# Routing the second feed-forward in segments of 20 and 12 token tiles

## Chip, cores and metric

One core of a Trainium2 chip. The metric is the device time of one execution in microseconds; the kernel before and the changed one run on the same chip, and the median of several runs counts.

## The reference

The input is 4096 tokens of 128 features. `x` goes through a macaron block:

```
x = x + 0.5 * ffn(layernorm(x))
x = x + attention(layernorm(x))
x = x + 0.5 * ffn(layernorm(x))
```

`ffn` is a mixture of 8 experts with top-2 gating:

```
weights = softmax(x @ gate_w.T + bias); top_w, top_i = top_k(weights, 2); top_w /= sum(top_w) + 1e-6
for e in range(8):
    h = gelu(x @ w_up[e].T)            # 128 -> 512
    out += sparse_w[..., e] * (h @ w_down[e].T)
out = layernorm(out) + x
```

`attention` is a causal linear attention (cosformer, 16 heads of 64, sequences of 1024 tokens) with ReLU features weighted by cos and sin of the position, a denominator, and an output projection.

## The kernel before

**Tiles.** 4096 tokens are 32 tiles of 128, or 8 blocks of 4 tiles. Tensors that the experts multiply are split into a high and a low f16 part.

**Segments.** Each feed-forward is routed in two segments of 16 tiles. Segments are numbered 0 and 1 (first feed-forward), 2 and 3 (second); even ones use `xs[0]`, `ys[0]` and half 0 of `slot_idx`, odd ones `xs[1]`, `ys[1]` and half 1. `gating` (L489) picks the two experts of each token in ten pieces (0 to 9) on VectorE, with an Exp on ScalarE after piece 0. `route_product` counts on TensorE, and `route` (L566), 20 operations on VectorE, computes where each (token, choice) goes, `slot_idx`, and which expert each tile of slots has, `tile_e`, packed three bits apiece into registers' words. `scatter` (L626) sends each tile's rows to DRAM `xs` in expert order, with two indirect DMAs a tile on GpSimd's queue. Each expert's rows are padded to 256, so a segment of 16 tiles (4096 rows) has 23 pairs of slot tiles, `NPAIR`.

**The pair loop.** For each pair, SP loads `xs` into one of three `xs_in` (L930), TensorE transposes it (L727), VectorE copies it (L824), TensorE multiplies (L742 to L744), ScalarE does gelu (L803) and the high part (L808), VectorE the low part (L828), TensorE the second product (L757 to L759), VectorE copies y into one of three `y_sb` (L835), SP stores it in `ys` (L936). SP's queue is in order: in iteration p it issues the load of pair p + 3 and then the store of pair p - 3. The loads of segment 1 or 3 start within the loop of the segment before, and the first of them waits for all scatters of its segment:

```
if p == 0:
    sp.wait_ge(scat[i % 2], 16 * 2 * HALF * (k + 1))
```

**After the pairs.** For each block q, GpSimd gathers each token's two rows from `ys` (`gather`, L665, eight indirect DMAs), VectorE combines and normalises (`combine`, L681 to L698), GpSimd takes the power (`finish_power`, L672), VectorE applies it and adds to x (`finish_apply`, L705, L710), SP stores the output. The blocks of segment 2 are done beside the pairs of segment 3 (combine in iterations 6, 10, 14, 18, apply in 9, 13, 17, 21); those of segment 3 after the last pair. `add_input` (L643) adds the normalised input to `x_tok` on GpSimd, one instruction per segment.

**Attention.** Blocks n = 0 to 7, each with 8 steps (hp = 0 to 7) of two heads. In each step GpSimd makes a low part of q (L1377, POOL), low parts of the state (L1380, L1381) and the products with cos and sin (L1359, two), VectorE multiplies scores by the decay (L1258), updates the state (L1271), makes the low part of the probabilities (L1275) and key features (L1233, `k_features`), and more. Other work is put into given steps by hand, in `beside` on VectorE and after the step on GpSimd:
- the layer norm before the second feed-forward of block n - 1 in steps 1 and 2 of block n, its transposes in 4 and its gate logits in 5;
- the gathers of the first feed-forward's last four blocks, one a step in blocks 0 to 3;
- the gating of segment 2 in block 5, its `route` in step 0 of block 6, its scatters from step 1 of block 6 to step 7 of block 7, one tile a step (two in the first).

The gating of segment 3 runs in iterations 4 to 8 of segment 2's pair loop, after block 7's layer norm, its `route` in iteration 10 and all its scatters behind that on GpSimd's queue.

## Time and profile before

| | |
|---|---|
| median of 3 runs | 1253.76 us (1251.31 to 1256.22) |
| profiled execution | 1257.42 us |
| its span, first to last instruction | 1255.5 us |
| busy: VectorE, TensorE, GpSimd, ScalarE | 1009.6, 928.8, 765.9, 707.3 us |
| mean granted clock of TensorE | 0.929 |
| attention, first L1377 to last | 288.5 to 993.8 us |
| second feed-forward, first low part to end | 1012.2 to 1255.5 us |

Times inside the execution are counted from the first instruction. The page calls the engines PE (TensorE), DVE (VectorE), ACT (ScalarE), POOL (GpSimd) and SP (SyncE). Share of busy time is a mean over stretches with different limits, so each stretch is read by itself. The row of a waiting instruction names, in brackets, how long its engine was idle and which instruction or DMA released it.

### The profile page before, as it was taken

The numbers are of one execution on the slowest core, as the hardware profiler recorded it, in microseconds if no ns is written. First come the engines' busy times: TensorE is split into PE (matmuls) and PEld (weight loads), VectorE is DVE, ScalarE is ACT, GpSimd is POOL, SyncE is SP. The second block draws the span as 40 slices with busy tenths as digits, with TensorE's granted clock in tenths as the row PEclk, the third lists the DMA queues.
The fourth block names the chain that finished last, engine by engine and source line by source line (L and its number), as shares of the span: only waits on it lengthen the run. The fifth ranks groups of instructions, "written<-read, shape, count | busy, mean of one in ns | idle before, by whom it ended". The sixth has DMA issues, their size and how long they took to land.

```text
span 1255.5 us, 32918 instructions
## 1 busy us (share of the span) xinstructions
PE 928.8 (74%) x12872; PEld 752.7 (60%) x12872; DVE 1009.6 (80%) x2109; ACT 707.3 (56%) x1014; POOL 765.9 (61%) x635
## 2 busy tenths in 40 slices
PE   3303988878988878878878988978979778859800
PEld 3302977766766656656656766756766667748700
DVE  7887786987889899899899898898888768538923
ACT  2112766657765755666765776746757646636600
POOL 2178736706867656757656565557987721767264
PEclk9999999989999998999999999988989989969955
DMA  9322424310000000000000000000000012234231
GB/s 336 128 109 73 141 79 111 103 47 6 8 9 8 8 6 8 8 7 8 8 6 2 2 2 2 2 2 19 14 14 13 21 53 72 95 97 122 77 93 50
DMA packets 69508, 61.77 MB, mean 49 GB/s; under 512 B 8304, under 2 KB 60016, under 8 KB 69104
## 3 DMA queue, kind: packets, MB, share of 16 engines
q1 hardware_dynamic: 60448, 42.64, 11.1%
q0 software_dynamic: 8192, 16.79, 4.3%
q8 instruction: 109, 1.79, 0.6%
q10 hardware_dynamic: 720, 0.23, 0.1%
q14 instruction: 39, 0.32, 0.1%
HBM read 30.80 MB, written 28.84 MB: 48 GB/s over the span
## 4 chain that ended last, share of the span: by engine, by line
DVE 30%; POOL 25%; PE 20%; issue 16%; ACT 6%; DMA 2%; DVEq 0%; POOLq 0%; SPq 0%
POOL xs L636 8%; POOL arena_a L1377 5%; DVE arena_b L1275 4%; POOL arena_a L1359 4%; DVE arena_a L1233 3%; PE bank L1043 3%; DVE arena_c L828 3%; ACT arena_c L1153 3%; POOL arena_b L665 2%; DVE arena_c L1271 2%; POOL arena_c L1381 2%; DVE xn_new L426 2%; DVE arena_b L1258 2%; PE bank L742 2%; DVE zt L705 2%
## 5 line engine op out<-in xcount | busy, mean ns | idle before, releaser
L636 POOL DMA_INDIRECT xs<-xhl,slot_idx x128 | 154.1, 1204 | 98.3 <-issue 57.2
L803 ACT ACTIVATE arena_c<-bank,s_pre 128x1024 f32<-128x1024 f32 x92 | 102.3, 1112 | 164.4 <-PE bank L744 158.9
L1377 POOL TENSOR_TENSOR arena_a<-arena_a 128x1024 f16<-128x1024 f32 x64 | 139.4, 2178 | 53.5 <-ACT arena_a L1153 52.9
L1359 POOL TENSOR_TENSOR arena_a<-arena_b,trig_rows 128x512 f32<-128x512 f32 x128 | 160.3, 1272 | 8.6 <-issue 8.6
L1153 ACT ACTIVATE arena_c<-arena_a 128x1024 f16<-128x1024 f32 x64 | 67.6, 1057 | 161.5 <-DVE arena_a L1233 161.5
L757 PE MATMUL bank<-wdn_hi,arena_c 128*128 x736 | 131.2, 222 | 31.8 <-DVE arena_c L828 31.8
L665 POOL DMA_INDIRECT arena_b<-ys,slot_idx x96 | 108.5, 1130 | 66.5 <-DMA ys<-arena_b 38.8
L828 DVE SCALAR_TENSOR_TENSOR arena_c<-arena_c,s_h 128x1024 f16<-128x1024 f32 x92 | 125.2, 1361 | 22.1 <-ACT arena_c L808 22.1
L758 PE MATMUL bank<-wdn_hi,arena_c 128*128 x736 | 131.2, 222 | 0.0
L759 PE MATMUL bank<-wdn_lo,arena_c 128*128 x736 | 131.0, 222 | 0.0
L1258 DVE TENSOR_TENSOR arena_b<-bank,decay 128x512 f32<-128x512 f32 x128 | 82.4, 686 | 41.0 <-PE bank L1043 40.4
L1153 ACT ACTIVATE arena_b<-arena_b 128x512 f16<-128x512 f32 x128 | 77.9, 630 | 63.9 <-DVE arena_b L1258 63.9
L808 ACT ACTIVATE arena_c<-arena_c,s_h 128x1024 f16<-128x1024 f32 x92 | 105.7, 1148 | 3.0
L742 PE MATMUL bank<-arena_b,wup_hi 128*128 128x256 f16 x368 | 103.9, 282 | 0.8
L743 PE MATMUL bank<-arena_b,wup_hi 128*128 128x256 f16 x368 | 103.8, 282 | 0.0
L744 PE MATMUL bank<-arena_b,wup_lo 128*128 128x256 f16 x368 | 103.7, 282 | 0.0
L1380 POOL TENSOR_TENSOR arena_c<-arena_c 128x130 f16<-128x130 f32 x64 | 35.6, 556 | 107.9 <-ACT arena_c L1203 107.6
L1275 DVE TENSOR_TENSOR arena_b<-arena_b 128x1024 f16<-128x1024 f32 x64 | 101.4, 1584 | 0.0
L1233 DVE SCALAR_TENSOR_TENSOR arena_a<-bank,trig_cols 128x512 f32<-128x512 f32 x128 | 82.3, 683 | 19.0 <-PE bank L969 18.0
L757 PEld LDWEIGHTS bank<-wdn_hi,arena_c 128*128 128x128 f16 x736 | 73.2, 99 | 35.2 <-issue 34.1
L967 PE MATMUL bank<-wo_hi,arena_c 128*128 128x128 f16 x256 | 49.4, 228 | 59.6 <-DVE arena_c L1242 59.5
L727 PE MATMUL bank<-ident_h,arena_b 128*128 128x128 f16 x368 | 37.5, 227 | 67.1 <-DMA arena_b<-xs 42.7
(227 smaller groups left out, 3762.8 us busy)
## 6 DMA issues: line engine op xcount, KB each, us to landing
arena_b<-xs SPq DMA_DIRECT2D x92, 128.0 KB
ys<-arena_b SPq DMA_DIRECT2D x92, 128.0 KB
xs<-arena_c SPq DMA_DIRECT2D x2, 3072.0 KB, 18.2
arena_a<-in_w_up SPq DMA_DIRECT2D x1, 2048.0 KB, 13.0
arena_b<-in_w_down SPq DMA_DIRECT2D x1, 2048.0 KB, 13.6
xs<-xhl,slot_idx POOLq DMA_INDIRECT x128, 2.3
out_x<-x_tok SPq DMA_DIRECT2D x8, 256.0 KB, 2.7
arena_b<-ys,slot_idx POOLq DMA_INDIRECT x96
```

Source lines behind the costliest of these rows:

```text
L636: nc.gpsimd.indirect_dma_start(d["xs"][half], bass.IndirectOffsetOnAxis(slot_idx[:, half, choice, t:t + 1], axis=0), xhl[:, half, t, :], N ...
L665: nc.gpsimd.indirect_dma_start(rows_of(q)[:, t, choice, :], None, d["ys"][half], bass.IndirectOffsetOnAxis(slot_idx[:, half, choice, at:at ...
L742: nc.tensor.matmul(dst, w_hi, x_hi, start=True, stop=False)
L757: nc.tensor.matmul(dst, hi, w_hi, start=(c + s == 0), stop=False, skip_group_check=True)
L758: nc.tensor.matmul(dst, lo, w_hi, start=False, stop=False, skip_group_check=True)
L759: i = nc.tensor.matmul(dst, hi, w_lo, start=False, stop=(c + s == CH), skip_group_check=True)
L828: nc.vector.scalar_tensor_tensor(h_lo[G % 4], h32[G % 2], s_h[:, 0:1], h_hi[G % 4], ALU.mult, ALU.subtract).then_inc(f["lo_done"], 1)
L1153: nc.scalar.activation(dst, src, ACT.Copy, scale=scale).then_inc(done, 1)
L1233: i = nc.vector.scalar_tensor_tensor(to[:, :, g, :], keys, 0.0, trig, ALU.max, ALU.mult)
L1275: nc.vector.tensor_tensor(probs_lo, probs, probs_hi, ALU.subtract).then_inc(a["probs_lo_done"], 1)
L1359: i = nc.gpsimd.tensor_tensor(q_trig[h], q_relu[h], trig_rows[:, bass.ds(u * BLK, BLK)], ALU.mult)
L1377: nc.gpsimd.tensor_tensor(q_lo, arena_a[:, 0:2 * BLK], q_hi, ALU.subtract).then_inc(a["q_lo_done"], 1)
```

## The change

The four segments get sizes of their own, in blocks 4, 4, 5, 3. The second feed-forward's segment 2 has 20 tiles and 27 pairs, segment 3 has 12 tiles and 19 pairs; the sum of pairs stays 46. Everything that was written with `HALF` or `NPAIR` uses `SEG_TILES`, `PAIRS` and `FIRST_PAIR`. The tables of `route` grow from 24 to 32 entries, and the zeroed scratch in DRAM from 24 to 28 pairs of tiles a half. The constants of routing stay in one SBUF tensor and aren't copied apart.

In attention, piece 0 of segment 2's gating moves from step 0 to step 6 of block 5 (block 4's gate logits must be in), the other pieces to steps 0 to 3 of block 6, `route` to step 4 of block 6, and the scatters to two tiles (four DMAs) a step from step 5 of block 6 to step 6 of block 7. In the pair loop, the fifth block of segment 2 is combined in iteration 22 of segment 3 and applied in iteration 25; three blocks are left for the end. TensorE waits for the last copy of y before it starts the attention.

```diff
-SLOTS, NPAIR, NTABLE = 24 * 2 * P, 23, 24
+SEG_BLOCKS = (4, 4, 5, 3)
+SEG_TILES = tuple(TPB * n for n in SEG_BLOCKS)
+SEG_START = (0, SEG_TILES[0], 0, SEG_TILES[2])
+SEG_END = (4, 8, 13, 16)
+PAIRS = tuple(n + E - 1 for n in SEG_TILES)
+FIRST_PAIR = (0, PAIRS[0], PAIRS[0] + PAIRS[1], sum(PAIRS[:3]), sum(PAIRS))
+SLOTS, NTABLE, WIDEST = 28 * 2 * P, 32, max(SEG_TILES)
...
             if j == 0:
-                v.wait_ge(gate_read, NBLK // 2 * (i + 1))
+                v.wait_ge(gate_read, SEG_END[i])
...
-        def spread(p, lag):
-            return p >= lag and (p - lag) % 4 == 0 and (p - lag) // 4 < NBLK // 2
+        def spread(p, lag, i):
+            return p >= lag and (p - lag) % 4 == 0 and (p - lag) // 4 < SEG_BLOCKS[i - 1]
...
             if k:
-                for q in range(NBLK + EARLY, 2 * NBLK):
+                for q in range(SEG_END[2], SEG_END[3]):
                     combine(v, q)
                     finish_apply(v, q)
...
                 ln_power(g, 1, NBLK - 1)
                 add_input(g, 2)
-                scatter(g, 3, range(0, HALF))
+                scatter(g, 3, range(0, SEG_TILES[3]))
                 add_input(g, 3)
+                for i in (2, 3):
+                    first = SEG_END[i] - SEG_BLOCKS[i]
+                    gather(g, first)
+                    for q in range(first + 1, SEG_END[i]):
+                        gather(g, q)
+                        finish_power(g, q - 1)
+                    finish_power(g, SEG_END[i] - 1)
...
                 if p == 0:
-                    sp.wait_ge(scat[i % 2], 16 * 2 * HALF * (k + 1))
+                    sp.wait_ge(scat[i % 2], 16 * 2 * (SEG_TILES[i] + (SEG_TILES[i - 2] if i > 1 else 0)))
...
             pe.wait_ge(w_att_ready, 1)
+            pe.wait_ge(f["y_used"], FIRST_PAIR[2])
...
-                if n == 5:
-                    for j in ((0,), (), (1, 2), (3, 4), (5, 6), (7,), (8,), (9,))[hp]:
+                if n == 5 and hp == 6:
+                    gating(v, 2, 0)
+                if n == 6 and hp < 4:
+                    for j in ((1, 2), (3, 4, 5), (6, 7), (8, 9))[hp]:
                         gating(v, 2, j)
-                if n == 6 and hp == 0:
+                if n == 6 and hp == 4:
                     route(v, 2)
...
-                        at = 8 * (n - 6) + hp - 1
-                        if at >= 0:
-                            scatter(g, 2, (at + 1,) if at else (0, 1))
+                        at = 2 * (NHP * (n - 6) + hp - 5)
+                        if 0 <= at < SEG_TILES[2]:
+                            scatter(g, 2, range(at, min(at + 2, SEG_TILES[2])))
...
-            nc.vector.tensor_copy(slot_tile[:], route_raw[:, 0:at])
-            nc.vector.tensor_copy(keep[:].rearrange("p e t -> p (e t)"), route_raw[:, at:at + E * NTILE // 2])
-            nc.vector.tensor_copy(below_b[:], route_raw[:, at + E * NTILE // 2:at + E * NTILE // 2 + P])
-            nc.vector.tensor_copy(digit[:], route_raw[:, at + E * NTILE // 2 + P:]).then_inc(const_ready, 1)
+            nc.vector.tensor_copy(below_b[:], below).then_inc(const_ready, 1)
```

## Rows read from the trace of the kernel before

**Rows 1.** Windows: stretch, length, busy us (instructions) by engine, clock, DMA.

```profile
288.50:363.40 74.90, 71.66 (x1126) 54.08 (x1123) 61.41 (x113) 57.34 (x96) 60.61 (x49) 1.00 0.03 8
...
734.20:820.70 86.50, 75.76 (x1142) 57.70 (x1142) 77.80 (x150) 60.48 (x104) 50.98 (x43) 0.98 0.01 2
820.70:917.30 96.60, 80.00 (x1172) 60.52 (x1169) 86.33 (x154) 59.93 (x102) 73.00 (x58) 0.93 0.03 12
917.30:993.80 76.50, 66.56 (x993) 50.80 (x991) 67.39 (x115) 51.62 (x88) 63.31 (x53) 0.96 0.04 14
...
1012.20:1090.20 78.00, 65.52 (x819) 59.32 (x817) 58.82 (x118) 51.52 (x48) 28.68 (x22) 0.93 0.25 75
```

**Rows 2.** Timeline of POOL, one step of block 6: start, us, engine, line.

```profile
877.02 2.15 POOL L1377 TENSOR_TENSOR arena_a<-arena_a 128x1024 f16<-128x1024 f32 x1
...
883.97 1.83 POOL L636 DMA_INDIRECT xs<-xhl,slot_idx  x1
886.11 0.96 POOL L636 DMA_INDIRECT xs<-xhl,slot_idx  x1 [0.30 <-issue]
887.09 2.13 POOL L1377 TENSOR_TENSOR arena_a<-arena_a 128x1024 f16<-128x1024 f32 x1
```

**Rows 3.** Waits of SP's queue: us in total, times, longest.

```profile
SPq L930 <- DMA xs<-xhl,slot_idx: 35.7, 2, 26.0
```

**Rows 4.** Timeline of VectorE from segment 2 to 3.

```profile
1087.28 1.28 DVE L828 SCALAR_TENSOR_TENSOR arena_c<-arena_c,s_h 128x1024 f16<-128x1024 f32 x1 [0.23 <-ACT arena_c L808]
...
1090.15 1.28 DVE L828 SCALAR_TENSOR_TENSOR arena_c<-arena_c,s_h 128x1024 f16<-128x1024 f32 x1 [0.56 <-ACT arena_c L808]
1109.95 0.42 DVE L835 COPY arena_b<-bank 128x256 f32<-128x256 f32 x1 [18.52 <-DMA ys<-arena_b]
...
1121.85 1.28 DVE L828 SCALAR_TENSOR_TENSOR arena_c<-arena_c,s_h 128x1024 f16<-128x1024 f32 x1 [1.68 <-ACT arena_c L808]
```

**Rows 5.** Timeline of VectorE from segment 0 to 1, same operations.

```profile
184.08 1.28 DVE L828 SCALAR_TENSOR_TENSOR arena_c<-arena_c,s_h 128x1024 f16<-128x1024 f32 x1 [0.57 <-ACT arena_c L808]
...
196.55 1.29 DVE L828 SCALAR_TENSOR_TENSOR arena_c<-arena_c,s_h 128x1024 f16<-128x1024 f32 x1 [1.68 <-ACT arena_c L808]
```

**Rows 6.** Timeline of VectorE near the end of segment 3.

```profile
1179.12 0.87 DVE L681 TENSOR_SCALAR zt<-arena_b,w 128x128 f32<-128x128 f32 x4
...
1182.52 0.17 DVE L698 TENSOR_SCALAR fvar<-fmv 128x4 f32<-128x4 f32 x1
...
1188.96 1.11 DVE L705 TENSOR_SCALAR zt<-zt,fmv,frstdh 128x128 f32<-128x128 f32 x4
...
1194.04 0.42 DVE L835 COPY arena_b<-bank 128x256 f32<-128x256 f32 x1 [1.38 <-PE bank L759]
```

**Rows 7.** Timeline of POOL: first gathers of the first and the last block.

```profile
1197.09 1.02 POOL L665 DMA_INDIRECT arena_b<-ys,slot_idx  x1 [13.32 <-DMA ys<-arena_b]
...
1229.42 1.01 POOL L665 DMA_INDIRECT arena_b<-ys,slot_idx  x1 [0.18 <-issue]
```

**Rows 8.** Timeline of VectorE in block 6: first and last of route, then L1275.

```profile
825.76 0.28 DVE L581 COPY rt_tot<-bank 128x128 f32<-128x128 f32 x1
...
833.71 0.17 DVE L605 CAST tile_e<-rt_pack 128x3 int32<-128x3 f32 x1
...
852.43 7.43 DVE L1275 TENSOR_TENSOR arena_b<-arena_b 128x1024 f16<-128x1024 f32 x1
```

**Rows 9.** Line L1275 over the whole span: duration ns min/median/max.

```profile
L1275 DVE TENSOR_TENSOR arena_b<-arena_b x64: 1212/1216/7435, 291.9 to 994.6; 128x1024 f16<-128x1024 f32 x64
```

**Rows 10.** Timeline of POOL: scatters 1, 24 and 32 of segment 3.

```profile
1061.53 1.99 POOL L636 DMA_INDIRECT xs<-xhl,slot_idx  x1 [40.80 <-DVE tile_e L605]
...
1095.10 0.96 POOL L636 DMA_INDIRECT xs<-xhl,slot_idx  x1 [0.30 <-issue]
...
1105.18 0.96 POOL L636 DMA_INDIRECT xs<-xhl,slot_idx  x1 [0.30 <-issue]
```

**Rows 11.** Timeline of VectorE at the start of the second feed-forward.

```profile
1016.30 5.29 DVE L426 TENSOR_SCALAR xn_new<-x_tok,mv,rstdh 128x128 f32<-128x128 f32 x4
```

More of the change, by code:

```diff
@@ L880, in ffn_pool @@
         def ffn_pool(g, k):
-            def finishing(q, power, norm):
-                gather(g, q)
-                if power is not None:
-                    finish_power(g, power)
-                if k == 0 and norm is not None:
-                    ln_power(g, 0, norm % 8)
             if k == 0:
@@ L891, in ffn_pool @@
                 reduce_largest(g, 2, 9, 2)
[L892 to L893 removed]
+                scatter(g, 0, range(10, SEG_TILES[0]))
+                scatter(g, 1, range(0, SEG_TILES[1]))
                 add_input(g, 0)
                 add_input(g, 1)
+                gather(g, 0)
+                for q in range(1, EARLY):
+                    gather(g, q)
+                    finish_power(g, q - 1)
+                    if q > 1:
+                        ln_power(g, 0, q - 2)
+                ln_power(g, 0, EARLY - 2)
+                finish_power(g, EARLY - 1)
+                ln_power(g, 0, EARLY - 1)
             else:
```

258 lines of the change are left out of this document (127 added, 131 removed).

## Prediction

> **What bounds the kernel now.** I read the table of windows first, then the chain of waits, then the timelines of GpSimd (POOL) and VectorE (DVE) around the places that the diff touches. Three stretches matter, and each has another limit.
>
> The attention runs 8 blocks of 8 steps. A block without gating, layer norm or scatters takes 74.9 us, so 9.4 us a step; block 5, which carries the gating of segment 2, takes 86.5, block 6, with its routing and 16 scatters, 96.6, and the first seven steps of block 7 take 76.5 [rows 1]. In the steps with two scatters the chain of waits stays on POOL without a gap: one step is 10.07 us from one subtraction L1377 to the next, and the scatters start 6.95 us into it [rows 2]. So POOL sets the pace there.
>
> The second feed-forward loses most at the change from segment 2 to 3. SP waited up to 26.0 us in one piece for scatters before it could issue a load [rows 3], and the stores queue behind that load. VectorE's low part of pair 21 starts at 1090.15, the first of segment 3 at 1121.85, with an 18.52 us wait for a store in between [rows 4]. The same passage in the first feed-forward, where the scatters were long done, takes 196.55 - 184.08 = 12.5 us [rows 5]. So 31.7 - 12.5 = 19.2 us are a stall.
>
> The last stretch is the gathers of four blocks on POOL after the last copy of y at 1194.04; the first starts at 1197.09, that of the fourth block at 1229.42 [rows 6, 7].
>
> **Start of the kernel.** Larger tables (32 instead of 24 entries, a wider `keep`), 7 MB instead of 6 MB zeroed, three small copies less on VectorE. The copies stood in front of a wait for TensorE's gate products, so they return nothing; the zeroing is waited for only by the first scatter, long after. The routing has two wider operations: +0.2 us. The new wait of attention_pe on the 46th `y_used` is implied already: TensorE has by then transposed block 3, whose layer norm stands behind the last copy of y on VectorE's queue. Nothing is queued behind it that could go earlier: 0. A fourth register load per segment: below 0.2 us, 0 taken.
>
> **Attention, block 5.** Nine of its ten pieces of gating leave, piece 0 stays and comes later. After that the block lies between 74.9, a block with neither gating nor layer norm, and 86.5. I take two thirds of the difference, because the layer norm stays: -7.8 us.
>
> **Attention, block 6.** It gets the gating (20 tiles for 16, in steps 0 to 3), the routing moves from step 0 to step 4, scatters from step 5. It looks like block 5 of before (86.5) plus the routing plus three steps with four scatters. The routing occupied VectorE from 825.76 to 833.88, 8.1 us [rows 8]; wider operands add 0.7 (estimate, a quarter more on some ten operations), and the clearing of s_run that block 6 has and block 5 hasn't 0.9. A scatter is 1.26 us where nothing disturbs it: the last eight started in 1105.18 - 1095.10 = 10.08 us [rows 10]. Two more in a step of 10.07 make 12.6. Three such steps replace ones of some 9.9: +8.1. Sum 86.5 + 9.7 + 8.1 = 104.3; with 9.4 for the replaced ones it is 105.8. I take 104.6, so +8.0 against 96.6. That the routing stands in a queue of VectorE in step 4 delays k_features and with it ScalarE, GpSimd and TensorE alike, as it did in step 0; nothing hides it in either place.
>
> **Attention, block 7.** Steps 0 to 6 carry four scatters for two. POOL alone: 7 x 12.6 = 88.2; before plus 7 x 2.52 = 94.1. POOL was busy 63.31 of 76.5 us [rows 1], and part of the idle 13.2 is a wait for VectorE that a later POOL no longer meets. I take 89.8: +13.3. The bounds are +11.7 and +17.6. A step could also be shorter than 12.6: in the step of [rows 2] the first scatter took 1.83 for 0.96, because VectorE was using its operands then; if the shifted phase avoids that, 0.9 less a step, 9 us less over the ten steps with four scatters. Step 7 has no scatters left, so the first load of the feed-forward is no longer behind them; at most 1 us, taken as 0.
>
> Attention in all: -7.8 + 8.0 + 13.3 = +13.5, bounds +4 and +20.
>
> What holds VectorE back in such steps is seen in the trace: at 852.43 its L1275 took 7.43 us, until POOL had run four operations in a row, and at 1016.30 L426 took 5.29 us beside the add of x_tok [rows 8, 11]. The Trainium skill (GPSIMD Engine Reference, Key points) says that GpSimd shares its SBUF interfaces with VectorE, and instructions with two SBUF inputs or in a 2-port mode contend. Taken for every step that rule would speak against this change, as below in the second rival; taken as the rows show it, now and then, it changes nothing in the sum, because a step of 12.6 us leaves VectorE about 3 us.
>
> **Segment 2, 27 pairs.** From its first low part to that of pair 21 it is 78.0 [rows 1]. add_input(2) gets 20 tiles, and VectorE waited 5.29 us beside it with 16 [rows 11]: +1.2. Gating of 12 tiles for 16: -0.6 (estimate). Four more pairs at 1090.15 - 1087.28 = 2.87: +11.5. Then the passage. The routing ends as before at pair 10, and the first scatter starts at 1061.53; 24 of them instead of 32, so the last starts at 1095.10 and has landed at about 1098.3 [rows 10]. The 32nd had landed at about 1105.18 + 2.2 = 1107.4, so SP came to the load at about 1107.4 - 26.0 = 1081.4, and it would come four pairs later, at 1092.9. It waits 5.4 us with the stores behind it. Before, VectorE first missed a store at 1109.95 - 18.52 = 1091.4, 10.0 us after SP was stuck; so 5.4 is hidden, by three y buffers, and what is next late is nothing. If that cover failed, each us over 10 would be lost once. The passage then costs 12.5. add_input(3), formerly inside the stall, now meets VectorE at work: +2.0 (estimate; nothing if it falls well, 3.6 at most, three quarters of the 4.8 us that the add beside L426 took). Sum 78.0 + 1.2 - 0.6 + 11.5 + 12.5 + 2.0 = 104.6, against 1121.85 - 1012.2 = 109.7: -5.1.
>
> **Segment 3, 19 pairs, and the end.** Before, from 1121.85 to the end of the span 133.7. Now the 19th low part ends where the combine starts, 1179.12 - 1121.85 = 57.3 after the start [rows 6]. Behind it on VectorE: the combine of the fourth block (1182.69 - 1179.12 = 3.6), two copies of y (0.9), the apply (1.11 and an add of 0.7, 1.8), and the combine of the fifth block (3.6), then POOL's power (about 1.2): 68.4 to 69. Only then may POOL gather block 13, since its queue has the fifth block's power ahead of it; that is 4 us later than its stores would allow. I take 68.9. Three blocks took POOL 1229.42 - 1197.09 = 32.3, so two take 21.5 [rows 7], and from the last one's start to the end it is 1255.5 - 1229.42 = 26.1. Sum 116.5: -17.2. Of this 11.5 are the four pairs that went to segment 2.
>
> **Sum.** 0.2 + 13.5 - 5.1 - 17.2 = -8.6 us. The profiled execution took 1257.42 us for a span of 1255.5, and the three timed runs have a median of 1253.76; I subtract from that: 1245.2.
>
> **The rivals.**
> First, cheap scatters: attention costs only +5, since collisions vanish with the shifted phase, and the rest as above: -17, 1237. For it speaks the idle time of POOL in block 7, against it that the steps with two scatters are POOL without a gap [rows 2]. Chance 0.13.
> Second, VectorE starved: a POOL that never idles keeps VectorE from its two-input subtraction, as at 852.43 for about 6 us [rows 8], not once but in most of the ten steps. Then each is some 14 us and not 12.6 (6 us, of which 3 are slack and half comes back), +14 to +20: 1262. It makes the change a loss of over 0.5% from 1.5 us a step. For it: the 7.43 us one follows the only step in which this kernel issues four scatters (the first two tiles of segment 2). Against it: the median of the 64 such subtractions is 1.216 us [rows 9]. Chance 0.08. The rule of the Trainium skill quoted above would make this the common case, and the time 1262.
> Third, the stall stays in part: if the routing or the scatters of segment 3 come 10 us later relative to the pairs, because gating at pairs 4 to 10 or scatters run slower, half of the 19.2 stays: 1254. The scatter times speak against it, with 5 us to spare [rows 10]. Chance 0.12.
> Fourth, no effect: the attention loses all that the feed-forward wins, with blocks 6 and 7 at their upper bounds: 1251 to 1254. Chance 0.15.
> My forecast, 1241 to 1249, has 0.52.
>
> **How the numbers follow.** The measurement tells about 0.5%, 6.3 us, from no change. Below 1247.5 lie four fifths of the forecast's 0.52, the first rival, and some of the third and fourth: 0.58. Above 1260: 0.09. Between: 0.33. The range for 8 in 10 leaves out the better half of the first rival and the second: 1236 to 1256; the forecast's own is 1241 to 1249.
>
> **What would show it.** Steps of block 7 near 12.6 us with four scatters; the sequence L1377 without idle. L1275 seldom above 2.4 us. No wait of VectorE's L835 for a store; SP's longest wait for scatters near 5. The passage near 12.5. The first gather of block 13 some 7 us behind the last copy of y, and three blocks of gathers at the end, not four. It would be wrong if POOL's steps are far from 12.6, if the routing in step 4 costs more than 8.8, or if the passage still has a gap.

## The result and the profile after

The changed kernel takes 1261.05 us (median of 16 runs, 1257.73 to 1266.48), the kernel before 1256.01 us on the same chip (16 runs, 1250.01 to 1262.2). The ratio is 1.0041, with a 95% interval from 1.0023 to 1.0059: about 5 us slower, where 8.6 us less had been forecast. On another chip the ratio was 1.0035 [1.001, 1.006] (e5 below).

The profiled execution has a span of 1262.8 us. The table of windows of the kernel after, cut at GpSimd's first subtractions (start of block 5, of block 6, of its step 5, the last of block 7) and at VectorE's first low part of segment 3. The columns are those of [rows 1]:

```profile
735.49:815.59 80.10, 73.88 (x1144) 56.40 (x1144) 69.42 (x131) 61.02 (x104) 50.74 (x43) 1.00 0.01 2
815.59:886.75 71.16, 50.42 (x698) 38.50 (x695) 62.91 (x124) 35.53 (x61) 33.15 (x27) 0.89 0.01 1
886.75:1022.05 135.30, 105.28 (x1485) 82.78 (x1484) 99.91 (x167) 78.27 (x132) 108.13 (x92) 0.89 0.05 21
1022.05:1145.88 123.83, 98.50 (x1202) 87.92 (x1200) 79.39 (x145) 69.30 (x65) 47.85 (x36) 0.88 0.27 81
1145.88:1262.80 116.92, 53.85 (x719) 49.75 (x716) 77.69 (x230) 40.48 (x36) 75.85 (x67) 0.76 0.32 89
```

The third row is the ten steps with four scatters each. They take 135.3 us. The same cuts in the kernel before give 86.50, 66.39 and 106.66 us, together 259.55 as in [rows 1]; after it is 80.10 + 71.16 + 135.30 = 286.56. So the attention from block 5 to its last subtraction is 27.0 us longer. Against this stand segment 2 with the passage, 105.95 us from the first low part at 1039.93 (before 109.68), and segment 3 to the end, 116.92 (before 133.65). With 1.3 us more until block 5 and 0.5 less between attention and feed-forward, 1.3 + 27.0 - 0.5 - 3.7 - 16.8 = 7.3 us, the difference of the two spans. The feed-forward gave what was forecast, and the attention took all of it and more.

Timeline of VectorE at the passage from segment 2 to 3, the counterpart of [rows 4]:

```profile
1134.28 1.29 DVE L849 SCALAR_TENSOR_TENSOR arena_c<-arena_c,s_h 128x1024 f16<-128x1024 f32 x1 [0.56 <-ACT arena_c L829]
...
1137.24 0.42 DVE L856 COPY arena_b<-bank 128x256 f32<-128x256 f32 x1 [1.33 <-PE bank L780]
...
1145.88 1.28 DVE L849 SCALAR_TENSOR_TENSOR arena_c<-arena_c,s_h 128x1024 f16<-128x1024 f32 x1 [1.48 <-ACT arena_c L829]
```

From the last low part of segment 2 to the first of segment 3 it is 11.6 us, and no wait for a store stands between them. The counterpart of the 12.5 us of [rows 5] is counted from the last but one, pair 25 at 1131.40: 14.5 us. SP's waits over the second feed-forward, the counterpart of [rows 3] (us in total, how many, the longest):

```profile
SPq L954 <- DVE arena_b L856: 118.5, 44, 10.6
SPq L974 <- DVE x_tok L731: 44.2, 4, 21.0
SPq L948 <- PE bank L748: 23.5, 14, 9.1
SPq L948 <- DMA xs<-xhl,slot_idx: 10.5, 2, 5.8
```

The 5.8 us in the last row are the wait in front of segment 2. At the passage, from 1085 to 1147, the one wait for scatters is this, where the working gave 5.4 and the kernel before had 26.0:

```profile
SPq L948 <- DMA xs<-xhl,slot_idx: 4.7, 1, 4.7
```

The loss is seen in the timelines of step 0 of block 7. GpSimd first:

```profile
920.54 1.82 POOL L652 DMA_INDIRECT xs<-xhl,slot_idx  x1 [0.17 <-issue]
...
925.19 0.95 POOL L652 DMA_INDIRECT xs<-xhl,slot_idx  x1 [0.30 <-issue]
926.16 2.15 POOL L1397 TENSOR_TENSOR arena_a<-arena_a 128x1024 f16<-128x1024 f32 x1
928.24 0.43 POOL L1400 TENSOR_TENSOR arena_c<-arena_c 128x130 f16<-128x130 f32 x1
928.61 0.89 POOL L1401 TENSOR_TENSOR arena_c<-arena_c 128x390 f16<-128x390 f32 x1
929.45 2.48 POOL L1379 TENSOR_TENSOR arena_a<-arena_b,trig_rows 128x512 f32<-128x512 f32 x2
939.10 1.27 POOL L1385 TENSOR_TENSOR x_tok<-x_tok,bo_row 128x512 f32<-128x512 f32 x1 [7.17 <-DVE x_tok L1371]
```

VectorE in the same step:

```profile
924.67 1.34 DVE L1289 SCALAR_TENSOR_TENSOR arena_c<-bank,arena_c 128x130 f32<-128x130 f32 x4
925.92 7.09 DVE L1293 TENSOR_TENSOR arena_b<-arena_b 128x1024 f16<-128x1024 f32 x1
932.94 1.27 DVE L1251 SCALAR_TENSOR_TENSOR arena_a<-bank,trig_cols 128x512 f32<-128x512 f32 x2
```

VectorE's subtraction L1293 (before: L1275) begins at 925.92, while GpSimd ends its fourth scatter. At 926.16 GpSimd begins its first arithmetic operation, and three more follow without a gap until 931.93. L1293, whose median is 1.216 us, ends only at 933.01, 1.08 us after GpSimd's last: it got nowhere until GpSimd was through. Everything behind it on VectorE, then TensorE, then GpSimd is late: the step takes 20.04 us. I call this a hold. It is the thing of [rows 8]. In the ten steps after there are two, at 925.92 and at 994.91 (6.62 us), and a third of L437 (4.58 us at 958.68), which is L426 of [rows 11].

Holds weren't rare in the kernel before either; most were short. In one more place a subtraction was held long, in block 2, and in the ten steps an operation of the layer norm was, both behind GpSimd's four operations in a row:

```profile
473.83 6.23 DVE L1275 TENSOR_TENSOR arena_b<-arena_b 128x1024 f16<-128x1024 f32 x1
...
930.72 5.44 DVE L414 TENSOR_SCALAR var<-mv 128x4 f32<-128x4 f32 x1
```

And in the step of [rows 2], VectorE's and GpSimd's next operations were these:

```profile
877.89 2.37 DVE L1275 TENSOR_TENSOR arena_b<-arena_b 128x1024 f16<-128x1024 f32 x1
...
879.23 1.30 POOL L1380 TENSOR_TENSOR arena_c<-arena_c 128x130 f16<-128x130 f32 x1
```

The subtraction began 0.87 us behind L1377 and ended 1.09 us behind its end (879.17). It was held for the first of GpSimd's operations only and went through ahead of the second, which then took 1.30 us instead of 0.43. Of the 14 subtractions beside a first subtraction of GpSimd that follows scatters, ten were longer than 1.3 us, nine of them by at most 1.23 us. The median of all 64 [rows 9] hides this. So what is new is not the hold but how often it is long.

### The profile page after: what moved, and what is told of

It reads as the page before. It is cut to its first block, busy times and chain, and to the rows that moved or that the text cites. A ratio compares the mean times of both kernels' runs of the same rounds, so it can differ in the third digit from the quotient of the medians.

```text
span 1262.8 us, 32926 instructions
## 1 busy us (share of the span) xinstructions
PE 940.0 (74%) x12872; PEld 764.5 (61%) x12872; DVE 1007.7 (80%) x2106; ACT 709.3 (56%) x1014; POOL 765.1 (61%) x635
## 4 chain that ended last, share of the span: by engine, by line
DVE 29%; PE 25%; POOL 21%; issue 16%; ACT 7%; DMA 1%; DVEq 0%; POOLq 0%; SPq 0%
POOL xs L652 6%; POOL arena_a L1397 5%; DVE arena_b L1293 4%; DVE arena_a L1251 3%; POOL arena_a L1379 3%; DVE arena_c L849 3%; PE bank L1062 3%; ACT arena_c L1172 3%; DVE arena_c L1289 2%; PE bank L763 2%; PE bank L765 2%; POOL arena_c L1401 2%; PE bank L764 2%; DVE xn_new L437 2%; PE bank L778 2%
## 5 line engine op out<-in xcount | busy, mean ns | idle before, releaser
L1397 POOL TENSOR_TENSOR arena_a<-arena_a 128x1024 f16<-128x1024 f32 x64 | 139.9, 2185 | 66.3 <-ACT arena_a L1172 65.8
L849 DVE SCALAR_TENSOR_TENSOR arena_c<-arena_c,s_h 128x1024 f16<-128x1024 f32 x92 | 128.6, 1398 | 22.1 <-ACT arena_c L829 22.0
L686 POOL DMA_INDIRECT arena_b<-ys,slot_idx x96 | 111.1, 1157 | 58.0 <-DMA ys<-arena_b 30.1
L778 PE MATMUL bank<-wdn_hi,arena_c 128*128 x736 | 132.6, 223 | 13.5 <-DVE arena_c L849 13.5
L1276 DVE TENSOR_TENSOR arena_b<-bank,decay 128x512 f32<-128x512 f32 x128 | 82.4, 686 | 50.7 <-PE bank L1062 50.1
L985 PE MATMUL bank<-wo_hi,arena_c 128*128 128x128 f16 x256 | 53.0, 238 | 67.7 <-DVE arena_c L1260 67.7
L1400 POOL TENSOR_TENSOR arena_c<-arena_c 128x130 f16<-128x130 f32 x64 | 30.4, 475 | 115.2 <-ACT arena_c L1222 115.2
L1293 DVE TENSOR_TENSOR arena_b<-arena_b 128x1024 f16<-128x1024 f32 x64 | 94.2, 1472 | 0.1
L1062 PE MATMUL bank<-arena_b 64*128 64x128 f32 x1024 | 86.3, 316 | 0.0
## 6 DMA issues: line engine op xcount, KB each, us to landing
arena_a<-in_w_up SPq DMA_DIRECT2D x1, 2048.0 KB, 13.5
```

The lines of the kernel that those rows point to most:

```text
L778: nc.tensor.matmul(dst, hi, w_hi, start=(c + s == 0), stop=False, skip_group_check=True)
L849: nc.vector.scalar_tensor_tensor(h_lo[G % 4], h32[G % 2], s_h[:, 0:1], h_hi[G % 4], ALU.mult, ALU.subtract).then_inc(f["lo_done"], 1)
L1293: nc.vector.tensor_tensor(probs_lo, probs, probs_hi, ALU.subtract).then_inc(a["probs_lo_done"], 1)
L1397: nc.gpsimd.tensor_tensor(q_lo, arena_a[:, 0:2 * BLK], q_hi, ALU.subtract).then_inc(a["q_lo_done"], 1)
```

## The experiments

"Attention" below is the time from GpSimd's first subtraction of block 5 to the last of block 7. It has three parts: block 5; steps 0 to 4 of block 6; and the ten steps from step 5 of block 6 to step 6 of block 7. All are differences of starts of L1397 (L1377) in the timelines.

| kernel | scatters a step in the ten | block 5 | steps 0 to 4 | ten steps | attention | ratio to before |
|---|---|---|---|---|---|---|
| before | 2 (10 more in steps 1 to 4, 2 in step 7 of block 7) | 86.5 | 66.4 | 106.7 | 259.6 | 1 |
| after | 4 | 80.1 | 71.2 | 135.3 | 286.6 | 1.0041 |
| e1 | 4, with a wait | 80.2 | 69.2 | 142.9 | 292.2 | 1.0188 |
| e2 | 2 | 80.2 | 71.0 | 108.3 | 259.4 | 0.9958 |
| e3 | 4 in eight | 80.1 | 68.3 | 124.0 | 272.4 | 1.0178 |
| e4 | 2 + 2 | 80.1 | 66.5 | 126.3 | 272.8 | 1.0017 |
| e5 (after again) | 4 | 80.1 | 70.3 | 130.8 | 281.1 | 1.0035 |
| e6 | 4 in eight | 87.1 | 57.9 | 128.2 | 273.2 | 1.0085 |
| e7 | 2 or 4, in twelve | 80.3 | 72.5 | 126.0 | 278.8 | 1.0008 |
| e9 (e4 again) | 2 + 2 | 80.1 | 71.2 | 125.3 | 276.7 | 0.9969 |
| e10 | 2 or 4, parted, in twelve | 80.3 | 68.7 | 123.9 | 272.8 | 0.9986 |
| e11 | 3 | 80.2 | 71.2 | 126.6 | 277.9 | 1.0003 |
| e12 | 1 + 1 | 86.3 | 63.0 | 104.2 | 253.5 | 0.9961 |

My theory after reading the trace: four scatters a step leave GpSimd no pause, so that VectorE's two-source subtraction is held again and again. The rivals: GpSimd's plain work; the gating and routing, moved and packed into five steps of block 6; TensorE's clock.

How plain work and waiting share the loss is read from GpSimd's timeline of the ten steps. The scatters have the 0.3 us with them that stand in front of each:

| kernel | scatters a step | ten steps | arithmetic | scatters | idle |
|---|---|---|---|---|---|
| before | 2 | 106.7 | 64.6 | 30.6 | 11.5 |
| e2 | 2 | 108.3 | 64.3 | 30.8 | 13.2 |
| e11 | 3 | 126.6 | 62.9 | 43.5 | 20.1 |
| after | 4 | 135.3 | 61.2 | 57.8 | 16.4 |
| e5 (after again) | 4 | 130.8 | 61.0 | 57.1 | 12.7 |
| e9 | 2 + 2 | 125.3 | 61.0 | 59.1 | 5.2 |

Against e2, which has the same schedule and half of the scatters, after is 27.0 us longer, and its 20 scatters more take 27.0 us. So the first rival, plain work, is right for what was added. The theory is right for what did not help to pay for it: with four scatters GpSimd still stands idle for 13 to 16 us, and only where they are parted (e9) is this slack used.

e1 to e4 ran on a chip on which the kernel before took 1344.59 us. Its feed-forward has gaps that the other chips don't show, in every kernel (104.9 to 107.1 us in e1 to e4, 76.0 in the kernel after, from the first low part of segment 0 to that of segment 1), while block 5 takes the same 80.1. So these four are read by their attention steps. There is no profile of the kernel before from that chip, and the ratios of e1 and e3 rest on four executions each.

**e1, GpSimd waits for VectorE.** Edit, behind the scatters of a step:

```
 scatter(g, 2, range(at, min(at + 2, SEG_TILES[2])))
+g.wait_ge(a["probs_lo_done"], s + 2)
```

> The kernel after, with one wait more: in each step that issues four scatters GpSimd waits, behind the fourth, until VectorE has written the low part of the probabilities of the next step. The operations are the same; only GpSimd can no longer run its four arithmetic operations over VectorE's two-source subtraction. Theory (starvation: four scatters a step keep GpSimd busy without a pause, and a subtraction of VectorE that begins with the first of GpSimd's operations is held until the fourth ends): the 6 to 7 us subtractions at 925.92 and 994.91 are gone, block 7's first seven steps take 88 to 92 us instead of 95.9, block 6 takes about 108, and the time falls by 5 to 9 us, to 1252 to 1256. Rival, plain work (GpSimd's queue is simply full, each scatter costs what it costs): the wait adds to a full queue, steps of 12.5 to 13.5 us, time the same or up to 5 us more. Rival, backlog of the moved gating and routing in block 6: block 7 changes little and block 6 stays at 110.

The ratio is 1.0188 [1.0122, 1.0254]. In these steps the holds of L1293 are gone, as the theory wanted; the ten steps take 142.9 us, as it did not. GpSimd's timeline in one step:

```profile
1019.11 1.02 POOL L652 DMA_INDIRECT xs<-xhl,slot_idx  x1 [0.15 <-issue]
...
1023.01 0.96 POOL L652 DMA_INDIRECT xs<-xhl,slot_idx  x1 [0.31 <-issue]
1027.62 2.12 POOL L1397 TENSOR_TENSOR arena_a<-arena_a 128x1024 f16<-128x1024 f32 x1 [3.65 <-DVE arena_b L1293]
```

GpSimd stands idle for 3.65 us here until VectorE is through, and starts this step 14.49 us after the last. In eight of the ten steps the gap is 1.1 to 3.7 us, 22.7 us in all, and the ten steps are 7.6 and 12.1 us longer than in the two executions without the wait. The hold that it prevents comes two times in ten. As a remedy the theory failed; that a hold needs GpSimd's arithmetic beside it was borne out.

**e2, half of the scatters.** The second choice of segment 2 isn't scattered:

```
-for choice in range(2):
+for choice in range(1 if i == 2 else 2):
```

> The kernel after, with only the first choice of each token of segment 2 scattered: two DMAs in each of the ten steps instead of four. The rows of the second choice are left out, so the output isn't the reference's. It prices the twenty scatters left out, with the schedule of gating and routing as it is after. Theory (scatters, by their own time and by the starvation that they bring): ten steps shorter by 2.5 us of plain work and by another 1 us of held subtractions, block 7's first seven steps 74 to 78 us instead of 95.9, block 6 about 101, attention from block 5 to its end 25 to 30 us shorter. Rival, backlog of gating and routing: block 6 stays above 106 with steps of 15 us around the routing, and at most 15 us come back in block 7. Rival, clock of TensorE: only if steps stay long although the scatters are halved.

The ten steps take 108.3 us, 10.8 a step: 27.0 less than in the profile of after, 22.5 less than in e5's. L1293 isn't held long, 2.36 us at most in the ten steps (one operation of the layer norm is, 5.45 us at 992.49). The rows of windows of e2, the second being gating and routing, the third the ten steps:

```profile
874.81:945.78 70.97, 50.12 (x698) 38.16 (x695) 63.07 (x124) 35.56 (x61) 33.19 (x27) 0.91 0.01 1
945.78:1054.05 108.27, 97.69 (x1468) 74.60 (x1466) 94.16 (x163) 76.10 (x129) 90.42 (x73) 0.98 0.04 14
```

Steps 0 to 4 of block 6 stay at 71.0: the backlog of gating and routing doesn't reach into the steps behind. The granted clock in the ten steps is 0.98 here and 0.89 after. Both are means of a stretch, between the two levels of 1.2 and 2.4 GHz. It comes back where the steps are short, at unchanged work for TensorE, and in e9 it is 0.94 with steps of 12.5 us; that speaks for a clock that follows the waits rather than makes them. Step by step it does not go with the length either: in after, the shortest step (11.14 us) has 0.73 and the steps of 15.69 and 15.07 us have 0.95 and 0.98, and in e9 two steps of 12.05 and 12.08 us have 0.72 and 1.00.

**e3, the new schedule with the old sizes.** `SEG_BLOCKS = (4, 4, 4, 4)`, `SEG_END = (4, 8, 12, 16)`.

> The schedule of the kernel after (gating one block later, routing in step 4 of block 6, four scatters a step) with the sizes of the kernel before: segments 2 and 3 of 16 token tiles each. It tells the price of the new schedule from that of the sizes. Eight steps have four scatters instead of ten. Theory: the attention costs nearly as much as after, some 22 to 27 us more than before from block 5 to the end, while the feed-forward loses the gain of the four pairs moved at the end (11.5 us, and 4 for an earlier last block); routing's stall at the passage between segments 2 and 3 returns in full. Time 1270 to 1280. Rival, that the sizes themselves cost (20 tiles of wider gating and scatters 17 to 20): attention only 15 us over that of before, time 1262 to 1268.

The ratio is 1.0178 [1.0126, 1.0231]; the attention takes 272.4 us, 13 more than before and not 22 to 27; the rival had 15. Those 13 us are 1.0% and not 1.8, and where the rest lies isn't known. Eight steps with four scatters take 105.9 us, the two without 18.0. No L1293 is above 2.7 us here, so this execution was also spared the long holds. The schedule with the old sizes makes about half of the attention's loss; that the two further steps, the wider gating and the holds make the rest is inferred, not tried one by one.

**e5, the kernel after once more.**

> The kernel after, unchanged, once more: how far do its step times repeat, and what is its time on this chip. If the held subtractions of VectorE are a matter of a few tenths of a microsecond in phase (theory, starvation by chance), the first seven steps of block 7 differ between executions by several microseconds: 95.9 the first time, 88 to 96 now, with other steps hit. If they come from the schedule itself (rival), they stand in the same steps again with the same 20.0 and 15.1 us. The ratio to before is 1.004 if the first comparison holds on this chip too.

Ratio 1.0035 [1.001, 1.006]. The ten steps take 130.8 us, the first seven of block 7 93.1 for 95.9, and the two holds of L1293 stand elsewhere, 6.29 us at 907.38 and 7.12 at 947.76:

```profile
947.76 7.12 DVE L1293 TENSOR_TENSOR arena_b<-arena_b 128x1024 f16<-128x1024 f32 x1
954.80 1.10 DVE L437 TENSOR_SCALAR xn_new<-x_tok,mv,rstdh 128x128 f32<-128x128 f32 x4
```

Its GpSimd operations run from 948.03 to 953.79 there, the last starting so:

```profile
948.03 2.14 POOL L1397 TENSOR_TENSOR arena_a<-arena_a 128x1024 f16<-128x1024 f32 x1
...
951.32 2.47 POOL L1379 TENSOR_TENSOR arena_a<-arena_b,trig_rows 128x512 f32<-128x512 f32 x2
```

Which step is hit is a matter of phase; step 0 of block 7 took 16.81 us here and 20.04 in the first execution. Between two executions of this kernel the attention differs by 5.4 us. The kernel before repeats better: in e8, where the attention is untouched, it takes 259.2 us for 259.6, and the long hold of block 6 stands in the same step (7.45 us at 852.15). Neither profile of the kernel after is of a middling execution: they took 1264.66 and 1253.60 us, against medians of 1261.05 and 1260.64.

**e6, the kernel before with its scatters packed.** Nothing else changes:

```
-at = 8 * (n - 6) + hp - 1
-if at >= 0:
-    scatter(g, 2, (at + 1,) if at else (0, 1))
+at = 2 * (NHP * (n - 6) + hp - 5)
+if 0 <= at < HALF:
+    scatter(g, 2, (at, at + 1))
```

> The kernel before, with nothing changed but the place of its 32 scatters of segment 2: not two a step in steps 0 to 7 of blocks 6 and 7, but four a step from step 5 of block 6 in eight steps. Sizes, gating and routing stay. It prices the concentration alone. Theory (two scatters a step fit into GpSimd's slack and cost about 1 us, the third and fourth cost their full 2.5 us and more): the eight steps with four take 12.6 to 13.5 us, the steps before them 0.9 to 2 less than before each; attention from block 5 to its end 8 to 13 us longer than before, time 1.007 to 1.010 of before. Rival, that gating and routing in block 6 are the larger part of the loss: attention only 0 to 4 us longer.

Ratio 1.0085 [1.0055, 1.0115], attention 273.2 us: 13.6 more than before for the same 32 scatters. The eight steps with four take 105.8 us, 13.2 each, and the long holds are back: 6.28 us at 915.53 and 6.63 at 983.69. Spread by two a step, scatters lie mostly in GpSimd's slack; packed, they don't. That alone is half of the loss of 27.0 us, and more of the 21.6 in e5.

**e7, gating and routing a step earlier, 40 scatters over twelve steps.**

```
+if n == 5 and hp == 7: gating pieces 1, 2
-if n == 6 and hp < 4:  ((1, 2), (3, 4, 5), (6, 7), (8, 9))[hp]
+if n == 6 and hp < 3:  ((3, 4, 5), (6, 7), (8, 9))[hp]
-if n == 6 and hp == 4: route(v, 2)
+if n == 6 and hp == 3: route(v, 2)
-at = 2 * (NHP * (n - 6) + hp - 5); tiles at, at + 1
+at = NHP * (n - 6) + hp - 4; tiles 5 * at // 3 to 5 * (at + 1) // 3
```

> The kernel after, with gating steps 1 and 2 in step 7 of block 5, the others in steps 0 to 2 of block 6, the routing in step 3 and the 40 scatters spread over twelve steps (three or four a step, two in none) instead of ten. Theory (the cost lies in scatters per step above two): the surplus over two a step falls from 20 to 16, so 2.5 to 6 us less than after, but the gating of two more pieces in step 7 of block 5 costs up to 1 us there: attention 2 to 5 us shorter than the kernel after on this chip. Rival, that VectorE's backlog from gating and routing sets the loss: no change, or worse because four pieces of gating now meet the add and layer norm of steps 0 and 2.

TensorE's product for the route moves a step earlier too. Each of the twelve steps in fact has two or four scatters, 3.3 on average. Ratio 1.0008 [0.9989, 1.0028], attention 278.8 us, 2.3 less than e5. The theory's range holds, at its lower end, though 2.3 us are less than the 5.4 between two executions of the kernel after; one long hold of L1293 is left (7.14 us at 909.65).

**e8, the kernel before with the store ahead of the load.**

```
 for p in range(NPAIR + 3):
+    if p >= 3:
+        store(NPAIR * i + p - 3)
     (the loads)
-    if p >= 3:
-        store(NPAIR * i + p - 3)
```

> The kernel before, with one edit on SP's queue: in each turn the store of a finished pair goes ahead of the load three pairs on, so no store stands behind a load that waits for scatters. Theory (of the 31.7 us between pair 21 and the first pair of segment 3, 18.5 are the wait for a store, and without it only the load itself is late): pairs 21 and 22 come without a gap and the first pair of segment 3 follows the last scatter by the load and its transposes; the passage takes 22 to 25 us instead of 31.7, 6 to 9 us less, ratio to before 0.993 to 0.996. Rival: the load's own lateness sets the passage, nothing is gained.

Ratio 0.9974 [0.9953, 0.9994], about 3 us and not 6 to 9. VectorE at the passage:

```profile
1092.28 1.29 DVE L828 SCALAR_TENSOR_TENSOR arena_c<-arena_c,s_h 128x1024 f16<-128x1024 f32 x1 [0.56 <-ACT arena_c L808]
1110.83 0.42 DVE L835 COPY arena_b<-bank 128x256 f32<-128x256 f32 x1 [17.26 <-DMA ys<-arena_b]
...
1118.44 1.28 DVE L828 SCALAR_TENSOR_TENSOR arena_c<-arena_c,s_h 128x1024 f16<-128x1024 f32 x1 [1.68 <-ACT arena_c L808]
```

Pair 22 came at 1092.28, before at 1110.29: one store got through, so one pair more came early; the next store stands behind the next load. From pair 21 (1089.63) to the first of segment 3 it is 28.8 us and not 22 to 25. And the last scatter issued at 1106.09 comes 12.35 us ahead of the first low part of segment 3: the load itself is late, whatever the stores do. The rival was right for all but one pair. In the kernel after, earlier scatters took the stall away; other orders of the queue weren't tried.

**e4 and e9, two scatters behind the first subtraction, two at the end of the step.** The same kernel on two chips:

```
 q_lo = relu_q - q_hi                       (first subtraction)
+scatter(g, 2, (at,))
 g.wait_ge(a["s_hi_done"], s + 1) ... s_lo, trig_q
-scatter(g, 2, range(at, min(at + 2, SEG_TILES[2])))
+scatter(g, 2, (at + 1,))
```

> The kernel after with its four scatters of a step parted: two behind GpSimd's first subtraction, two at the end of the step. GpSimd's work is the same, but two of its two-source operations no longer come back to back with the rest. Theory (held subtractions come from four GpSimd operations in a row): the 6 to 7 us cases shrink to 2 to 4 us, but the low part of the state comes 2.5 us later in each step, which TensorE waits for; together a gain of 0 to 6 us, 1255 to 1261. Rival, plain work and TensorE waiting for the state's low part: 5 to 15 us slower than after. If the order within a step doesn't matter at all, the same as after.

> The kernel after with the four scatters of a step parted, two behind GpSimd's first subtraction and two at the end, once more and beside runs of the kernel before on this chip. The first time its steps with four scatters took 12.6 us on average (13.5 and 13.0 in the two executions of the kernel after). Theory (long holds of VectorE come from GpSimd's work in a row, and parting it makes them short): ten such steps sum to 124 to 128 us, no subtraction of VectorE above 4 us, attention from block 5 to its end 272 to 275 us, ratio to before 0.994 to 1.000, against 1.004 for the kernel after. Rival, that the first time was luck: 281 to 287 us again and 1.004.

The ratios are 1.0017 [0.998, 1.0054] and, on a chip where the kernel before took 1257.02 us, 0.9969 [0.9948, 0.999]. The ten steps take 126.3 and 125.3 us, in e9 all behind step 0 between 12.05 and 12.41. e9's attention (276.7) missed the 272 to 275 I had set, because its steps 0 to 4 of block 6 took 71.2 again and not 66.5. 2.3 of these us lie in step 2, and they are a hold too. VectorE in e9 and in e4:

```profile
844.73 2.85 DVE L437 TENSOR_SCALAR xn_new<-x_tok,mv,rstdh 128x128 f32<-128x128 f32 x4
847.50 1.40 DVE L542 TENSOR_TENSOR gt<-gt,gcol 128x160 f32<-128x160 f32 x1
```

```profile
894.72 1.11 DVE L437 TENSOR_SCALAR xn_new<-x_tok,mv,rstdh 128x128 f32<-128x128 f32 x4
895.74 0.32 DVE L542 TENSOR_TENSOR gt<-gt,gcol 128x160 f32<-128x160 f32 x1
```

In e9 GpSimd's last three operations of the step began at 845.02, beside them, in e4 at 895.61, when L437 was nearly over. VectorE in a step of the ten, beside GpSimd's first subtraction, which ran from 948.76 to 950.91 in e9:

```profile
948.74 1.29 DVE L1276 TENSOR_TENSOR arena_b<-bank,decay 128x512 f32<-128x512 f32 x2 [2.20 <-PE bank L1062]
949.95 1.34 DVE L1289 SCALAR_TENSOR_TENSOR arena_c<-bank,arena_c 128x130 f32<-128x130 f32 x4
951.20 1.22 DVE L1293 TENSOR_TENSOR arena_b<-arena_b 128x1024 f16<-128x1024 f32 x1
952.33 4.81 DVE L437 TENSOR_SCALAR xn_new<-x_tok,mv,rstdh 128x128 f32<-128x128 f32 x4
```

And GpSimd behind it:

```profile
951.08 0.99 POOL L652 DMA_INDIRECT xs<-xhl,slot_idx  x1 [0.17 <-issue]
952.37 0.96 POOL L652 DMA_INDIRECT xs<-xhl,slot_idx  x1 [0.30 <-issue]
953.36 0.42 POOL L1403 TENSOR_TENSOR arena_c<-arena_c 128x130 f16<-128x130 f32 x1
...
954.57 2.49 POOL L1379 TENSOR_TENSOR arena_a<-arena_b,trig_rows 128x512 f32<-128x512 f32 x2
```

L1276 and L1289, which have one source in PSUM, run at their usual speed beside GpSimd's subtraction. L1293, with both sources in SBUF, falls into the time of the two scatters and takes 1.22 us. L437 runs into GpSimd's next three operations and is held until they end at 957.06. Parted scatters don't end the holds, they limit them: behind the first subtraction stands a scatter, so a subtraction of VectorE that meets it waits for that one operation. In e9 four of the ten steps have an L1293 of 1.56 to 2.36 us and none is above, in e4 the longest is 3.61.

**e10, both edits.**

> Both edits on the kernel after: gating and routing one step earlier with the 40 scatters over twelve steps, and one tile's scatters of each step behind GpSimd's first subtraction, the other's at the end of the step. If both gains are of separate kinds (fewer scatters a step; no long holds), attention from block 5 to its end takes 268 to 273 us and the ratio to before is 0.990 to 0.996, the fastest of all. If the price is only the number of scatters and GpSimd's plain work, nothing is gained beyond e9: 0.995 to 1.000.

Ratio 0.9986 [0.9966, 1.0006], attention 272.8 us, no L1293 above 2.41 us. The attention is 3.9 us shorter than in e9 and inside the range that was set for two separate gains, but the times don't show it: the ratio is above the 0.990 to 0.996 of that range, and its interval overlaps e9's.

**e11, three scatters a step.** The second choice of every odd token tile of segment 2 is left out: `for choice in range(1 if i == 2 and t % 2 else 2)`

> The kernel after with three scatters a step instead of four: the second choice of every odd token tile of segment 2 is left out, so a quarter of its rows are missing and the output isn't the reference's. With two a step ten such steps took 108.3 us, with four 135.3 and 130.5; without scatters they would take 99.9. Theory (a knee: the first two hide in GpSimd's slack, each further one costs its 1.27 us and starts the holds): three cost 119 to 123 us, near 12 us a step, with at most one hold above 5 us. Rival, that each scatter costs the same: 117. Rival, that only the fourth, where GpSimd has no pause left, brings the loss: 110 to 113.

126.6 us, above all that was expected. The longest hold is 7.26 us (L1293 over the whole span, duration ns min/median/max):

```profile
L1293 DVE TENSOR_TENSOR arena_b<-arena_b x64: 1212/1216/7262, 292.4 to 1008.7; 128x1024 f16<-128x1024 f32 x64
```

and two more are held long, 7.24 us at 971.16 and 4.82 at 1008.67, the last at the end of the ten. The theory had at most one above 5 us. So the ten steps cost 108.3 us with two, 126.6 with three, 130.8 and 135.3 with four: 1.8 us a step for the third scatter, 0.4 to 0.9 for the fourth. The knee is between two and three, where GpSimd's idle time rises from 13.2 to 20.1 us; the difference for the fourth is no larger than that between two executions. But the theory's reason for it, that GpSimd has no pause left, doesn't hold. In [rows 2] GpSimd has none either: its scatter ends at 887.07 and its subtraction begins at 887.09, and so it is in most steps of before and e2. What differs is where VectorE's subtraction falls. In the steps of 10.07 us it begins 0.87 to 1.68 us behind GpSimd's first each time and gets through behind that one. With three or four scatters it begins anywhere from 4.6 us ahead to 4.2 behind. All that were held for 6 us or more, in all runs, began between 0.61 us ahead and 0.65 behind; three others in that stretch with the same operations beside them (0.33, 0.41 and 0.55 us behind) got through after 2.67 to 2.91 us, and why isn't known.

**e12, the kernel before with parted scatters and the store ahead of the load.** The first choice's scatter goes behind the first subtraction, the second choice's stays at the end of the step, and e8's edit stands.

> The kernel before with the store ahead of the load (as in e8, ratio 0.997) and with its two scatters of a step parted: the first choice's behind GpSimd's first subtraction, the second choice's at the end of the step. Theory (parting helps only where three or four scatters stand in a row and set off holds of VectorE; two in a row set off one, in the step behind the routing): steps stay at 10.1 us, attention from block 5 to its end 255 to 260 us against 259.5, ratio 0.993 to 0.998. Rival, that parting shortens every step because a scatter beside VectorE's work runs faster: steps of 9.4 to 9.7, attention 250 to 254 us, ratio 0.989 to 0.993. Against both: the low part of the state comes 1.3 us later in each step, and TensorE waits for it: steps of 10.5 or more, ratio 1.000 or above.

Ratio 0.9961 [0.994, 0.9982], the lowest of the kernels that scatter all rows, though not apart from e8 or e9. It lies in the theory's range (0.993 to 0.998), but the attention takes 253.5 us, which is in the rival's 250 to 254 and below the theory's 255 to 260: the long hold of [rows 8] is gone, which gives 3.2 of the 6.1 us (24.0 to 20.8 over two steps), and most steps take 9.7 to 10.1 us against 10.07. In nine of the ten steps L1275 takes 1.22 us (3.56 in the tenth), so the short holds are gone too. Parting helps a little beyond the long holds.

## Why the prediction was wrong

The step that failed is the attention term, +13.5 us with bounds of +4 and +20: one duration of 12.6 us for every step with four scatters, and the gating priced as in block 5. It was +27.0 in the first profile of the changed kernel and +21.6 in e5's (281.12 - 259.55). The sum of the other terms held:

- **Segment 2 and the passage**: forecast 104.6, found 105.95. add_input(3) held one low part for 5.07 us instead of 1.28 and cost 5.66 + 1.84 - 2 x 2.87 = 1.8 us over two pairs, against the 2.0 taken. The passage, 12.5 in the sum, took 14.5 us from pair 25; TensorE's granted clock was 0.73 in its last 6.4 us, where it was 1.00 in the first feed-forward's. The rest of the stretch came out 0.6 us below the sum. SP's wait at the passage was 4.7 us for 5.4. The 5.4 had a slip in it: it counts a scatter as landed 3.2 us behind its start in one place (1095.10 to 1098.3) and 2.2 in the other (1105.18 to 1107.4); with 2.2 in both it is 4.4. The third rival is out.
- **Segment 3 and the end**: forecast 116.5, found 116.92. The first gather of block 13 started at 1216.06, 46.7 us ahead of the end; 21.5 + 26.1 = 47.6 was forecast.
- **Start**: first low part 0.7 us later, block 5 1.3 us later, forecast 0.2. In e5 block 5 began 3.1 us earlier than before, so this is within what executions differ by.

Inside the attention, the misses of the first profile and, behind them, of the second:

- Block 5: forecast 78.7, found 80.1: +1.4, +1.4.
- Gating and routing, steps 0 to 4 of block 6: forecast 104.6 - 3 x 12.6 = 66.8, found 71.2 and 70.3: +4.4, +3.5. The routing step was right: 18.02 against 9.19 us for step 4 of block 5 is +8.8, as forecast. The gating was mis-sized. I had priced it by what it cost block 5 of before. That is 86.5 - 80.1 = 6.4 us with one or two pieces in a step; with two or three pieces in a step, steps 0 to 3 take 53.1 us against 41.3 in block 5 of after, 11.8 more, of which 0.9 had been given to clearing s_run. VectorE is busy 47.5 us in these four steps and 37.5 in those of block 5.
- Steps 5 to 7 of block 6: 37.8 forecast, 39.4 and 37.7 found: +1.6, -0.1.
- First seven steps of block 7: 89.8 forecast, 95.9 and 93.1 found: +6.1, +3.3.

The sums are 13.5 and 8.1 us; the medians missed the forecast by 5.0 + 8.6 = 13.6.

For the steps with four scatters I took one duration, 12.6 us, and argued that the rule of the Trainium skill would change nothing because such a step leaves VectorE about 3 us. Measured, there are two kinds. Six of the ten steps of after took 11.1 to 12.3 us, 11.8 on average, less than forecast. The others are the one behind the routing and those with a hold or just behind one: 15.69, 20.04, 13.71 (L437) and 15.07. Of the 20.04 some 3 us belong to step 0 of any block (13.02 with two scatters, against 10.07 for its neighbours). The mean is 13.5, in e5 13.1. So the first rival (cheap scatters) was right for the undisturbed steps, where L1293 mostly takes 1.22 us and not the 2.37 of before. The second (VectorE starved) was right for two in ten rather than for most; its +1.5 us a step over 12.6 came out as +0.9 and +0.5. That its time of 1262 was nearly met is luck: of the miss, 5.8 of 13.5 us (4.9 of 8.1 in e5) lie in block 5 and the gating, where it had nothing. I had looked at the median of all 64 subtractions, which hides the short holds and says nothing of the long ones. Of the steps with four scatters the trace of before had one, behind the routing, and it was held [rows 8]. One out of one says little of a rate, but it was the only row of that kind, and I read it as an exception.

What the experiments say of the parts: parting the scatters (e9) takes away the long holds of L1293 and 5.5 to 10.0 us (130.8 and 135.3 to 125.3). The other 17 us over two scatters a step (125.3 - 108.3) are GpSimd's own work: 28.3 us more for scatters than in e2, 3.3 less for arithmetic and 8.0 less idle. Packing without any other change costs 13.6 us (e6).

Why the gating costs more when it is packed was not tried by an experiment of its own. A hold in step 2 is part of it: L437 and L542 take 2.81 and 1.40 us there in after, 1.11 and 0.32 in e4. What makes up the other half of the 4.8 us by which steps 0 to 4 of block 6 differ between e4 and e9, the same kernel, is open.

## What to carry to other kernels

Price work added to a paced engine by its slack in a step: up to there it costs a part of its own time (two scatters a step give 10.8 us, where the same steps of block 5 without scatters give 10.0), beyond it costs its full time and what it does to a neighbour (three, 12.7). Ask also how it shifts the two engines against each other: a hold that was short because of where an operation fell can become long. A single outlier in a trace is worth asking what was special around it, and whether the change makes that the rule. Where work has to stand on such an engine, part it, so that the neighbour's two-source operation finds a gap; the one wait tried here (e1) cost more than it saved.

## What the hardware showed

- A VectorE operation with both sources in SBUF made no headway while GpSimd did arithmetic. In the 14 traces of this case, all 128 subtractions L1275 or L1293 that began from 0.61 us ahead of GpSimd's first one to 1.8 behind it ended 1.1 to 1.2 us behind the end of that operation or of a later one in the same gapless run; alone it takes 1.216 us. Started from 0.27 us ahead to 0.58 behind, it took 7.09 us (925.92), 7.12 (947.76), 6.62 (994.91) and 6.29 (907.38). Those that began 0.7 us or more ahead took their 1.22 us.
- The wait goes the other way too: where VectorE got through first, GpSimd's next operation took longer, L1380 1.30 us instead of 0.43 (879.23).
- L437 shows the hold too, with one tile and per-partition scalars as sources, 4.81 us instead of 1.10, and so does the low part of the feed-forward, 5.07 instead of 1.28 beside one GpSimd add. Two operations with a source in PSUM were never slowed, beside GpSimd or not (after, ns min/median/max):

```profile
L1276 DVE TENSOR_TENSOR arena_b<-bank,decay x128: 678/681/693, 291.3 to 1018.1; 128x512 f32<-128x512 f32 x128
L1289 DVE SCALAR_TENSOR_TENSOR arena_c<-bank,arena_c x256: 281/293/296, 292.5 to 1019.8; 128x130 f32<-128x130 f32 x128
```

- The Trainium skill (GPSIMD Engine Reference, Key points) names the shared SBUF interfaces for instructions with two SBUF inputs or in a 2-port mode; the trace agrees for the subtractions, which have two, and adds how long. Whether L437 runs in such a mode no run here shows.
- Issuing scatters on GpSimd did not hold VectorE: in e9 L1293 took 1.22 us beside two of them.
- Two executions of the changed kernel, equal in all its work, put the long holds in other steps and differ by 5.4 us in the attention.
